# The long convolution of a gated transformer block: fp32 products in place of three fp16 products

## The reference

```
kv  = einsum('bhil,bhjl->bijhl', k_, v_)          # head_dim 8: products of channel pairs i, j
y   = irfft(rfft(kv, 2L) * rfft(ssm_kernel, 2L))[..., :L]   # causal convolution, L = 512
out = y + kv * D
out = einsum('bijhl,bhil->bjhl', out, q_)
x   = x + tanh(g_xattn[0]) * out
```

## Time and profile before

| what | value |
|---|---|
| median of 3 runs | 2119.79 us (2118.39 to 2122.4) |
| the profiled execution | 2123.9 us |
| its span in the trace | 2122.2 us |
| convolution stage | about the first 269 us of the span |
| mean clock granted to TensorE | 0.942 of full speed |
| TensorE busy | 1781.6 us (84%) |
| VectorE / ScalarE / GpSimd busy | 1263.2 / 860.1 / 437.6 us |

### The profile page before, as it was taken

How to read it: one execution, slowest core, us unless ns; L and a number is a source line. 1 busy time by engine, 2 the same in 40 slices (tenths; PEclk the granted TensorE clock), 3 DMA queues, 4 the chain that set the end, 5 groups by cost and what they waited for, 6 DMA issues and landing times. The chain is left out here.

```text
span 2122.2 us, 31609 instructions
## 1 busy us (share of the span) xinstructions
PE 1781.6 (84%) x11016; PEld 1051.1 (50%) x11017; DVE 1263.2 (60%) x2442; ACT 860.1 (41%) x1640; POOL 437.6 (21%) x332
## 2 busy tenths in 40 slices
PE   3989948998299997798887456999999999999998
PEld 2778823443166664354444123555555555555554
DVE  4978843331734343687786568474747474747473
ACT  3221123332222222333332246565656565656562
POOL 1324203333411112231321134202020101010100
PEclk9999969999599998899999777999999999999999
DMA  8222233332422223412300512000000000000000
GB/s 183 59 64 84 83 119 112 114 116 93 128 76 81 88 79 143 159 31 70 99 6 16 159 54 86 11 21 11 20 10 20 10 20 10 20 10 20 0 20 11
DMA packets 78731, 133.44 MB, mean 63 GB/s; under 512 B 6754, under 2 KB 31330, under 8 KB 78642
## 3 DMA queue, kind: packets, MB, share of 16 engines
q1 hardware_dynamic: 71488, 112.41, 16.6%
q0 software_dynamic: 5680, 18.62, 3.0%
q10 hardware_dynamic: 1474, 1.21, 0.2%
HBM read 100.94 MB, written 31.28 MB: 62 GB/s over the span
## 5 line engine op out<-in xcount | busy, mean ns | idle before, releaser
L1781 POOL TENSOR_TENSOR s_h_lo<-s_h,s_h_hi 128x512 f16<-128x512 f32 x32 | 37.0, 1155 | 420.9 <-DVE s_h_hi L2015 420.9
L1951 DVE TENSOR_REDUCE s_top<-s_lg 128x1 f32<-128x512 f32 x64 | 43.8, 686 | 130.0 <-ACT s_lg L1840 130.0
L2008 DVE SCALAR_TENSOR_TENSOR s_si_lo<-s_ring,s_si_hi 128x512 f16<-128x512 f32 x128 | 85.4, 685 | 58.8 <-ACT s_si_hi L1876 58.8
L463 PE MATMUL ring<-prod_hi,toep 128*128 128x288 f16 x320 | 93.8, 293 | 19.8 <-DVE terms L383 11.0
L274 POOL TENSOR_TENSOR prod_lo<-prod,prod_hi 128x2304 f16<-128x2304 f32 x16 | 73.3, 4578 | 170.9 <-ACT prod_hi L307 166.2
L1889 ACT ACTIVATE s_so_hi<-s_ring 128x512 f16<-128x512 f32 x128 | 76.9, 601 | 74.1 <-PE s_ring L2036 73.0
L2034 PE MATMUL s_ring<-w_mu_hi,s_xt_hi 128*128 128x512 f16 x256 | 99.0, 387 | 9.2 <-DVE s_xt_lo L1946 9.2
L2035 PE MATMUL s_ring<-w_mu_lo,s_xt_hi 128*128 128x512 f16 x256 | 98.8, 386 | 0.0
L2036 PE MATMUL s_ring<-w_mu_hi,s_xt_lo 128*128 128x512 f16 x256 | 98.7, 385 | 0.0
L2034 PE MATMUL s_ring<-s_ed_hi,s_xl_hi 128*128 128x512 f16 x256 | 97.9, 383 | 0.2
L2018 DVE TENSOR_TENSOR s_so_lo<-s_ring,s_so_hi 128x512 f16<-128x512 f32 x128 | 87.4, 683 | 17.7 <-ACT s_so_hi L1889 17.5
(11 more groups left out here) (402 smaller groups left out, 5206.7 us busy)
## 6 DMA issues: line engine op xcount, KB each, us to landing
expert_rows<-e_y SPq DMA_DIRECT2D x39, 256.0 KB, 2.0
toep<-ssm_split SPq DMA_DIRECT2D x14, 512.0 KB, 5.1
stage<-in_L_ffn_gate_w SPq DMA_DIRECT2D x8, 704.0 KB, 7.0
stage<-in_L_ffn_up_w SPq DMA_DIRECT2D x8, 704.0 KB, 7.0
c_rows<-in_ctx SPq DMA_DIRECT2D x8, 512.0 KB, 9.7
x_rows<-in_x SPq DMA_DIRECT2D x8, 512.0 KB, 13.6
res<-in_x SPq DMA_DIRECT2D x128, 32.0 KB
after_conv<-gated SPq DMA_DIRECT2D x128, 32.0 KB
```

The lines of the kernel that those rows point to most:

```text
L463: nc.tensor.matmul(out, w_hi, hi, start=(n == 0), stop=False)
L1951: V.tensor_reduce(top[:, t, j:j + 1], lg[:, t, j * D:(j + 1) * D], AX.X, ALU.max).then_inc(S["top_done"], 1)
L2008: V.scalar_tensor_tensor(si[1][:, j % 2, m, :], ring[:, bank, :], 1.0 / N, si[0][:, j % 2, m, :], ALU.mult, ALU.subtract).then_inc(S["si_l ...
```

## The change

Pair products and Toeplitz tiles stay fp32. A block product is one fp32 matmul on `prod` and the fp32 tile. The high and low copies, the casts on ScalarE, the subtractions on GpSimd and VectorE and their semaphores go. The scratch tensor holds fp32 rows; a tile is still 512 KB, as two rows of 2 KB for each partition where it had four rows of 1 KB. `convolve(s, 0)` waits for `prod_done` in place of `lo_done`, and `pairs(s)`, which overwrites the buffer that `convolve(s - 2, .)` reads, waits for all of `convolve(s - 2, .)`.

```diff
-def conv_stage(nc, k, x, ctx, ssm_reversed, ssm_d, g_xattn, g_ffn, ssm_split, x1):
+def conv_stage(nc, k, x, ctx, ssm_reversed, ssm_d, g_xattn, g_ffn, ssm_rows, x1):
...
-        ssm_q = sb("ssm_q", [SSM_H, 2, PAD], F16)
-        toep = sb("toep", [P, T_BUFS, 2, 2, D], F16)
+        toep = sb("toep", [P, T_BUFS, 2, D])
         prod = sb("prod", [P, 2, PAIRED * KD])
-        prod_hi, prod_lo = (sb(f"prod_{n}", [P, 2, KD, 2, B * PAIRS], F16) for n in ("hi", "lo"))
...
-            src = bass.AP(tensor=ssm_split.tensor, offset=s * (4 * PAD), ap=[[1, P], [PAD, 4], [1, D]])
-            eng.dma_start(toep[:, s % T_BUFS].rearrange("p e q d -> p (e q) d"), src).then_inc(toep_loaded[s % T_BUFS], 16)
+            src = bass.AP(tensor=ssm_rows.tensor, offset=s * (2 * PAD), ap=[[1, P], [PAD, 2], [1, D]])
+            eng.dma_start(toep[:, s % T_BUFS], src).then_inc(toep_loaded[s % T_BUFS], 16)
...
     (GpSimd)
-            for s in range(STEPS):
-                u = s % 2
-                pool.wait_ge(hi_done, s + 1)
-                if s >= 2:
-                    pool.wait_ge(conv_done, (s - 1) * KD)
-                nc.gpsimd.tensor_tensor(prod_lo[:, u].rearrange("p k e r -> p (k e r)"), prod[:, u, :],
-                                        prod_hi[:, u].rearrange("p k e r -> p (k e r)"), ALU.subtract).then_inc(lo_done, 1)
...
     (ScalarE)
-            nc.scalar.activation(ssm_q[:, 0, :], ssm[:, :], ACT.Copy).then_inc(ssm_hi, 1)
             nc.scalar.preload_act_table(ACT.Sqrt)
-            act.wait_ge(ssm_lo, 1)
-            act.dma_start(ssm_split.rearrange("s e q d -> e s (q d)"), ssm_q[:, :, :].rearrange("h q d -> h (q d)")).then_inc(ssm_stored, 16)
+            act.dma_start(ssm_rows.rearrange("s e d -> e s d"), ssm[:, :]).then_inc(ssm_stored, 16)
...
-            def split(s):
-                u = s % 2
-                act.wait_ge(prod_done, s + 1)
-                if s >= 2:
-                    act.wait_ge(conv_done, (s - 1) * KD)
-                nc.scalar.activation(prod_hi[:, u].rearrange("p k e r -> p (k e r)"), prod[:, u, :], ACT.Copy).then_inc(hi_done, 1)
-            split(0)
-            split(1)
-                if s + 2 < STEPS:
-                    split(s + 2)
...
     (VectorE)
-            dve.wait_ge(ssm_hi, 1)
-            nc.vector.tensor_tensor(ssm_q[:, 1, :], ssm[:, :], ssm_q[:, 0, :], ALU.subtract).then_inc(ssm_lo, 1)
...
     (pairs)
                 if s >= 2:
-                    dve.wait_ge(lo_done, s - 1)
+                    dve.wait_ge(conv_done, (s - 1) * KD)
...
     (TensorE)
+            def pairs_of(s, n, e):
+                return prod[:, s % 2, :].rearrange("p (k e r) -> p k e r", k=KD, e=2)[:, n, e, :]
...
-                    pe.wait_ge(lo_done, s + 1)
+                    pe.wait_ge(prod_done, s + 1)
...
-                        w_hi, w_lo = (toep[:, u, e, q, t:t + P] for q in range(2))
-                        hi, lo = (a[:, s % 2, n, e, :] for a in (prod_hi, prod_lo))
-                        nc.tensor.matmul(out, w_hi, hi, start=(n == 0), stop=False)
-                        nc.tensor.matmul(out, w_hi, lo, start=False, stop=False)
-                        last = nc.tensor.matmul(out, w_lo, hi, start=False, stop=(n == m))
+                        last = nc.tensor.matmul(out, toep[:, u, e, t:t + P], pairs_of(s, n, e), start=(n == 0), stop=(n == m))
...
-                   scratch("ssm_split", (SSM_H // 2, 2, 2, D + P), F16), x1.rearrange("(b n) d -> b n d", n=N))
+                   scratch("ssm_rows", (SSM_H // 2, 2, D + P)), x1.rearrange("(b n) d -> b n d", n=N))
```

More of the change, by code:

```diff
@@ L164, in conv_stage @@
             sem(n) for n in ("ident_zeroed", "ident_ready", "gates_loaded", "gates_ready", "zeroed"))
-        ssm_loaded, d_added, ssm_hi, ssm_lo, ssm_stored = (sem(n) for n in ("ssm_loaded", "d_added", "ssm_hi", "ssm_lo", "ssm_stored"))
+        ssm_loaded, d_added, ssm_stored = (sem(n) for n in ("ssm_loaded", "d_added", "ssm_stored"))
         loaded = {"c": [sem(f"c_loaded{u}") for u in range(2)], "q": [sem(f"x_loaded{u}") for u in range(2)]}
@@ L170, in conv_stage @@
         res_loaded, stored = [sem(f"res_loaded{u}") for u in range(2)], [sem(f"stored{u}") for u in range(2)]
-        prod_done, hi_done, lo_done = sem("prod_done"), sem("prod_hi_done"), sem("prod_lo_done")
+        prod_done = sem("prod_done")
         conv_done, weighed, summed, added = sem("conv_done"), sem("weighed"), sem("summed"), sem("x_added")
```

## The result

The changed kernel takes 2142.6 us (2141.83 to 2144.94) beside 2119.1 us of the kernel before, a ratio of 1.011 (95% interval 1.0092 to 1.0127). Measured a second time it gave 2141.45 beside 2121.1, 1.0103 (1.0086 to 1.012). So it is slower by 20 to 23 us, 1%. The forecast was 2133.5, with a range to 2150: the direction was right, and the rise was 23.5 us where 13.65 had been forecast.

The account below looks back on a forecast made before the run. In even steps a DMA loop of stores, loads and Toeplitz tile was taken to set the pace. Start -4.2, opening +2.6, even steps +12.9, last step +2.35 summed to +13.65 us on 2119.8: 2133.5 us, range 2122 to 2150.

Parts of the forecast that it names:

- The product: Convolution stage: one fp32 product of 288 columns takes 0.485 us, as two records, in place of 0.3675 for three fp16 products.
- (d): Rival for the convolution products: one record each, 0.242 us, so not slower, 2099 us in all; 4 in 100.
- (a): Rival for the convolution products: weight loads not hidden, 0.86 us per product, about 2255 us in all; 4 in 100.
- Even steps: Ten even convolution steps: TensorE takes over as the pace, 13.62 us of work per step, +12.9 us.
- tile loop: Even steps before the change: stores, loads and Toeplitz tile landing form a two-step loop of 24.52 us, 12.26 per step.
- The added wait: Pair products wait for all of an earlier convolution: 0.25 us slack in even steps, under 1 us in steps 2, 3, 5.
- The start: Before the first product: VectorE no longer sits out GpSimd's subtraction, first product from 50.59 to about 46.4, -4.2 us.
- Last step: Last convolution step and its tail: 20 products, each dearer by 0.1175 us, +2.35 us.
- (b): Rival for the convolution stage: fp32 products hold the clock at 1.2 GHz, 2330 us in all; 3 in 100.
- (c): Rival for the convolution steps: the new wait stretches each by 0.2 to 0.8 us, 2137 to 2148 us; 12 in 100.
- Opening: Convolution steps 0 to 4: dearer products against less idle time and less half clock, +2.6 us (0 to +9).
- (e): Rival for the opening: it gains 8 us and gives back all the products cost, 2123 us in all; 7 in 100.

Follow-up runs that it names:

- e6: Changed kernel with each fp32 product cut into two of 144 columns, weights loaded again for each half; 2145.6 us in a single run.
- e1: Kernel before (fp16), with Toeplitz tiles issued from ScalarE's queue instead of SyncE's behind stores and loads; 2118.0 beside 2122.8 us, ratio 0.9979.
- e7: Changed kernel with Toeplitz tiles issued from ScalarE's queue; 2141.7 us beside 2123.6 us of the kernel before, ratio 1.0095.
- e4: Changed kernel with three buffers for pair products in place of two; 2140.1 us beside 2122.8 us of the kernel before, ratio 1.0079.
- e3: Changed kernel with the fp16 copies, ScalarE casts and GpSimd subtractions put back but unread; 2145.5 us beside 2122.8 us of the kernel before, ratio 1.0106.
- e2: Kernel before (fp16), with GpSimd's subtractions of steps 0, 3 and 4 held back until VectorE's layer norms are done; 2120.1 beside 2122.8 us, ratio 0.9988.
- e8: Kernel before with seven small DMAs, each waited for, as a pause at the end of the convolution stage; 2133.65 beside 2123.6 us, ratio 1.0045.
- e9: Kernel before with fourteen small DMAs, each waited for, as a pause at the end of the convolution stage; 2143.96 beside 2121.1 us, ratio 1.0108.
- r1: The changed kernel measured and traced again without further edits; 2141.45 us beside 2121.1 us of the kernel before, ratio 1.0103.

## Why the prediction was right in the mechanism and short in the size

**The product.** 0.485 us forecast, 0.485 measured, as two records of 0.2425. L2051 was the right row to read, count of records and all. Rival (d), one record per product, is out with 640 records, and (a), loads in series, with the starts and with e6. The Trainium skill's rule that weight loads overlap only where row groups differ (TensorE: Matmul & The Clock Gate, Part 3, The mechanism) does not describe this trace: all loads use all rows, and no time is left for them. The same section also lets a load run ahead of running matmuls where it goes to the background weight buffer, which the prediction left out; that would fit the trace, though no run here can show which buffer a load took.

**Even steps.** +12.9 forecast, +14.1 measured. The pace went from the tile loop to TensorE as said (e1, e7): 12.26 to 13.64 us, where the products alone would have added 2.35. Of the missing 1.2 us, 1.0 is step 5, 14.65 us long: the last turn stands just ahead of it, and it has the gap of 0.75. I had counted it as even. The rest is 13.64 for 13.62. That longer pieces of the tile "can only help" did not come true, the median landing is 5.5 us for 5.1, but with TensorE as the pace it cost nothing (e7).

**The added wait.** I gave it 0.25 us of slack in an even step and got that. In the opening I priced it at under 1 us in three steps, and they show 0.73 to 0.75. With the slower restart behind each gap they cost 1.0 us apiece, 3.0 together (e4).

**The start.** -4.2 forecast for the silent GpSimd, 4.6 by e3. The removed casts ahead of the ssm store, which I said might give up to 1 us and set to nothing, gave about 1.3. Over three traces of each kernel (see the opening below) the first product moved from 51.0 to 44.6 in the mean, 6.4 us. That only an operation with two on-chip inputs sits out GpSimd's was too narrow (e2).

**Last step.** +2.35 forecast, +2.4 measured. Rivals (b) and (c) did not come: the clock is 1.00 in the even steps.

**Opening.** +2.6 forecast, +3.4 in the first pair of traces, and that it came so near is luck. The openings of two more traces of the kernel before (e8, e9) and of two more with fp32 products (e7, r1), from the first product to step 5:

```profile
51.10:129.13 78.03, 66.21 (x527) 55.81 (x526) 66.36 (x123) 23.71 (x40) 22.88 (x5) 0.93 0.22 63
51.29:128.49 77.20, 66.70 (x528) 56.62 (x527) 65.66 (x124) 24.23 (x41) 22.89 (x5) 0.94 0.22 62
...
44.48:129.91 85.43, 79.33 (x427) 65.24 (x427) 59.63 (x121) 13.45 (x35) 0.00 (x0) 0.93 0.23 62
44.51:129.73 85.22, 79.13 (x427) 65.12 (x427) 59.58 (x121) 13.46 (x35) 0.00 (x0) 0.93 0.23 64
```

With the first pair the means are 78.8 and 85.1 us, a rise of 6.3. I had TensorE's work at full clock at 61.4 us before and 73.2 after. Busy time above that, which is my estimate of what half clock cost, was 8.8, 4.8 and 5.3 us before and 3.2, 6.1 and 5.9 after. So half clock gave back about 1.2 us in the mean, where the forecast took 6.2 off (8.7 to 2.5) from one trace, the one with the most of it. The idle time fell by 4.3, for 3 forecast. Rival (e), that the opening pays for the products, is out.

The sum for the stage, 13.65, stands against 14.0 in the first two traces. **The step that fell short is the last one of the sum**, "the median of the runs is 4.1 lower, and I put the same 13.65 on it". A difference worked out from one execution was laid on a median, as if that execution's stage were the usual one. It was the longest of three: they end at 264.0, 266.8 and 268.7, mean 266.5, and three of the changed kernel (with e7) at 282.7, 283.3 and 283.4, mean 283.1. That is 16.6 us and not 14.0, and the difference lies in the opening, through its half clock.

The rest is smaller than the first pair of medians makes it. With the pauses of e8 and e9 taken off, the spans of the same six traces differ by 18.2 us in the mean. The medians of the kernel before went from 2119.1 to 2123.6 between sets of runs. All its 42 runs have a mean of 2122.3, the eight of the changed kernel 2142.1: 19.8 us. So 1.6 us lie between the stage and the span, and 1.6 more between six traces and all runs; the latter are not settled. The later phases run the same code. From the scaling of their first norm to the last product of L2034 (in the kernel before) twelve traces show 1828.2 to 1837.2 us. They were 1828.3 in the kernel before and 1831.5 in the changed one, and that accounts for the first traces' 17.9 (0.7 more lie in the first transfer of the next phase). e9 makes a cost of a later start unlikely, r1 a cost of the change in these phases.

## What to carry to other kernels

Before pricing a dearer product, find what paces its loop: here TensorE had 1 us of slack per step under a DMA loop, so 2.35 us of products cost 1.4, and on a kernel without that loop they would have cost all of it (11.28 in e1, 13.64 in e7). Removing hidden work can pay through what it blocked, and reading a buffer directly instead of a copy moves a wait to whoever refills the buffer: count what is queued behind it. And when a change is worth under 1%, read the stage in two or three executions before laying a difference on the median.

## What the runs showed of the hardware

- An fp32 product runs as two records of 0.2425 us for 288 columns and 0.1225 us for 144, at full clock: 0.84 to 0.85 ns per column and record, four times the fp16 time per column in all. Three fp16 products (0.3675 us) beat one fp32 product (0.485 us).
- Weight loads of fp32 last 0.19 us each in the trace, but in e6 they started every 0.1225 us, and two records of 144 columns took 0.245 us where one of 288 takes 0.2425.
- A VectorE addition of 128x4 elements with both inputs in SBUF, the engines' working memory, took 4.38 us beside a GpSimd subtraction and 0.17 us without. A VectorE scaling of 128x512 with one tile in SBUF took 3.37 us beside it and 0.54 without (e2). Instructions that read one input from PSUM, as the weighs, had a median of 1.046 us in the even steps of the kernel before, where the subtraction runs, and 1.037 us in those of the changed kernel (41 of each); the ten that began during a subtraction had 1.059.
